# Summing stage and the tail of the expert stage: the margins are zeroed first, gathers and row statistics stand earlier in the queues, and ScalarE's order in a chunk is changed

## What is computed

```python
x = x + _layernorm(_L0_ffn_ref(_layernorm(x), ...))     # experts
x = x + _layernorm(_L1_attn_ref(_layernorm(x), ...))    # state space

# end of the experts: a token's four expert outputs, weighted, and the shared part
routed = einsum('ne,nef,efd->nd', comb, g * u, wd)
return routed + shared

# start of the state-space layer
proj = x @ W_in.T
val, gate, Bp, Cp, dt = split(proj, ...)
vc = conv_general_dilated(val, conv_w, padding=[(3, 0)])   # 4 taps, causal
val = silu(vc + conv_b)
```

## Time and profile before

| | |
|---|---|
| median of 3 runs | 1275.85 us (1274.46 to 1279.34) |
| profiled execution | 1269.8 us, of which the span is 1268.0 us |
| PE, PEld busy | 88%, 72% of the span |
| DVE, ACT, POOL busy | 69%, 50%, 30% of the span |
| expert stage | ends at 504.57 us |
| summing stage | 504.8 to 631.0 us |
| busy in the summing stage, by engine | PE 58 to 80%, DVE 39 to 87% of its parts |
| TensorE clock granted | 0.93 over the span, 0.72 to 0.84 in the summing stage |

### The profile page before, as it was taken

The page is one execution under the profiler, slowest core; times in us unless marked ns, Lnnn a source line. Parts: engine busy times, 40 slices in busy tenths (PEclk is TensorE's granted clock), DMA queues, the critical chain, the costliest instruction groups (busy, mean ns, idle before and its releaser), DMA issues. The chain is left out here.

```text
span 1268.0 us, 31644 instructions
## 1 busy us (share of the span) xinstructions
PE 1115.9 (88%) x12161; PEld 915.7 (72%) x12161; DVE 871.2 (69%) x2188; ACT 630.3 (50%) x1433; POOL 386.6 (30%) x561
## 2 busy tenths in 40 slices
PE   6569998689989993676799999999999999999987
PEld 5446776577778993455557888888888888888776
DVE  6467896877846776685476677667766776664574
ACT  4434456232333663476644554555455555553654
POOL 3331222176700265672055016202620261000120
PEclk9869999777999996777899999999999999999998
DMA  6748884222289885463243234223342332232001
GB/s 175 187 118 223 214 232 176 104 82 89 84 325 419 300 301 169 124 184 119 100 102 102 85 111 125 85 85 114 122 151 89 116 116 87 91 102 80 1 18 50
DMA packets 77986, 176.17 MB, mean 139 GB/s; under 512 B 12614, under 2 KB 26182, under 8 KB 75270
## 3 DMA queue, kind: packets, MB, share of 16 engines
q1 hardware_dynamic: 71564, 157.09, 38.6%
q0 software_dynamic: 6272, 17.05, 4.4%
HBM read 112.82 MB, written 61.08 MB: 137 GB/s over the span
## 5 line engine op out<-in xcount | busy, mean ns | idle before, releaser
L2378 ACT ACTIVATE decay<-masked,negcum 128x128 f32<-128x128 f32 x512 | 163.0, 391 | 101.8 <-DVE mixT L2442 101.8
L2286 PE MATMUL joint<-xh,w_high 128*128 128x512 f32 x512 | 209.3, 409 | 2.0 <-POOL wl L2222 2.0
L2286 PE MATMUL joint<-xl,w_high 128*128 128x512 f32 x512 | 200.2, 391 | 0.0
L2286 PE MATMUL joint<-xh,wl 128*128 128x512 f32 x512 | 199.9, 390 | 0.0
L2490 DVE COPY cT<-joint 128x512 f32<-128x512 f32 x128 | 88.3, 690 | 85.9 <-PE joint L2286 85.6
L2396 ACT ACTIVATE bT<-joint 128x512 f32<-128x512 f32 x128 | 76.7, 599 | 131.1 <-PE joint L2286 131.1
L2442 DVE TENSOR_TENSOR mixT<-pcb,decay 128x512 f32<-128x512 f32 x128 | 82.5, 685 | 55.7 <-PE pcb L2302 55.6
L2219 POOL TENSOR_TENSOR w_high<-w_in,none 128x512 fp32r<-128x512 f32 x32 | 36.1, 1127 | 260.7 <-DMA w_in<-in_w_bc 251.3
L2286 PEld LDWEIGHTS joint<-xh,w_high 128*128 128x128 f32 x512 | 96.2, 188 | 23.7 <-POOL wl L2222 2.4
L2286 PEld LDWEIGHTS joint<-xh,wl 128*128 128x128 f32 x512 | 96.1, 188 | 20.8
L2286 PEld LDWEIGHTS joint<-xl,w_high 128*128 128x128 f32 x512 | 96.3, 188 | 17.0
(11 more groups left out here) (367 smaller groups left out, 2717.3 us busy)
## 6 DMA issues: line engine op xcount, KB each, us to landing
cumrow<-ssm_cum SPq DMA_DIRECT2D x128, 256.0 KB, 3.2
slots_in<-blank SPq DMA_DIRECT2D x16, 1024.0 KB, 5.3
rows<-slots_in SPq DMA_DIRECT2D x32, 512.0 KB, 5.4
slots_out<-spare SPq DMA_DIRECT2D x32, 512.0 KB, 4.2
weights<-in_expert_quads SPq DMA_DIRECT2D x16, 768.0 KB, 8.8
w_in<-in_w_bc SPq DMA_DIRECT2D x32, 256.0 KB, 3.8
qk_parts<-parts SPq DMA_DIRECT2D x32, 192.0 KB, 2.3
stack<-qk_parts SPq DMA_DIRECT2D x32, 192.0 KB, 5.2
```

What stands on the lines that cost most here:

```text
L2286: last = nc.tensor.matmul(bank[:], w[:, j, col:col + P], a[:, k, c * CHUNK:(c + 1) * CHUNK], start=(m == 0), stop=(m == len(parts) - 1))
L2378: last = nc.scalar.activation(decay[:, n % 2, o], masked[:, n % 2, o], ACT.Exp, bias=negcum[:, c * TPC + i, head:head + 1])
```

## The change

It moves instructions and adds or removes no computation.

```diff
-EARLY_FROM, EARLY_EACH = 24, 2
+EARLY_FROM, EARLY_EACH = 23, 2
-COMBINE_AT = [26, 28, 30, 32]
+COMBINE_AT = [25, 27, 29, 31]
@@ stage_slots, GpSimd
                         for n in range((g - EARLY_FROM) * EARLY_EACH, (g - EARLY_FROM + 1) * EARLY_EACH):
+                            if n == TPC * TOPK:
+                                stored(1)
                             fetch(n)
-                stored(1)
-                late = list(range(TPC * TOPK, EARLY_TILES * TOPK))
-                for n in late[:4]:
+                for n in range((NQ - EARLY_FROM) * EARLY_EACH, EARLY_TILES * TOPK - 2):
                     fetch(n)
                 deviations(OF_Y)
-                for n in late[4:6]:
+                for n in range(EARLY_TILES * TOPK - 2, EARLY_TILES * TOPK):
                     fetch(n)
                 deviations(OF_X)
-                for n in late[6:]:
-                    fetch(n)
@@ stage_slots, VectorE, in the loop over the quads
+                    if g == NQ - 1:
+                        for part in w_copied:
+                            dve.wait_ge(part, OVER // 2)
+                        dve.wait_ge(added, TPC * TOPK)
+                        statistics(y, OF_Y)
@@ stage_mid, GpSimd
+                nc.gpsimd.memset(pad[:, :, :, 0:TAPS - 1], 0.0).then_inc(padded, 1)
                 for i in range(EARLY_TILES, 9):
                     fetch(i)
                 link(nc.gpsimd.memset(power[:], -0.5))
-                nc.gpsimd.memset(pad[:, :, :, 0:TAPS - 1], 0.0).then_inc(padded, 1)
                 deviations(OF_Y, 1)
                 fetch(9)
                 deviations(OF_X, 1)
-                for i in range(10, 13):
+                for i in range(10, 15):
                     fetch(i)
                 deviations(OF_Y, 2)
-                fetch(13)
+                fetch(15)
                 deviations(OF_X, 2)
-                for i in range(14, NT):
-                    fetch(i)
@@ stage_mid, ScalarE
                 for c in range(LAST):
-                    take(c, range(CB_IN))
+                    take(c, range(CB_IN - 2))
                     for v in range(2):
                         silu(c, v)
+                    take(c, range(CB_IN - 2, CB_IN))
+                    normal_rows(c + 1)
                     for v in range(2):
                         values(c, v)
-                    normal_rows(c + 1)
                     high_part(c + 1)
```

More of the change, by code:

```diff
@@ L1430, in _ @@
                         for n in range((g - EARLY_FROM) * EARLY_EACH, (g - EARLY_FROM + 1) * EARLY_EACH):
+                            if n == TPC * TOPK:
+                                stored(1)
                             fetch(n)
-                for n in range((NQ - EARLY_FROM) * EARLY_EACH, TPC * TOPK):
-                    fetch(n)
                 pool.wait_ge(w_copied[1], OVER // 2)
                 link(nc.gpsimd.memset(norms["power"], -0.5))
-                stored(1)
-                late = list(range(TPC * TOPK, EARLY_TILES * TOPK))
-                for n in late[:4]:
+                for n in range((NQ - EARLY_FROM) * EARLY_EACH, EARLY_TILES * TOPK - 2):
                     fetch(n)
                 deviations(OF_Y)
-                for n in late[4:6]:
+                for n in range(EARLY_TILES * TOPK - 2, EARLY_TILES * TOPK):
                     fetch(n)
                 deviations(OF_X)
-                for n in late[6:]:
-                    fetch(n)
             @block.sync
```

## The result

The changed kernel takes 1267.04 us in the median of six runs (1262.39 to 1269.18). The kernel before, run on the same chip, took 1274.03 (1269.75 to 1279.34). The ratio is 0.9945, with a 95% interval of 0.9919 to 0.9970: faster by 0.55%. Forecast were 1269.7 us and a gain of 6.2. Measured against the runs beside it, the gain is 7.0; the kernel before had a median of 1275.85 in the three runs that the forecast started from and 1274.03 in six, which is 1.8 of the 2.7 us between forecast and result.

What follows compares the result with a forecast made beforehand. GpSimd's drain was taken to end the expert stage, a GpSimd-VectorE loop to pace the summing stage. Expert -6.2 and summing +0.1 + 0.3 - 0.4 = 0 took 1275.85 to 1269.7 us; range 1264.2 to 1275.6.

Steps and rivals of the forecast that it cites:

- VectorE: Expert stage: with the third combine no longer ahead of the last product, VectorE's statistics start 2.8 us earlier (1.8 to 3.3).
- The drain: End of the expert stage: with no gather behind the second power, GpSimd's drain ends 6.2 us earlier (4.2 to 8.3).
- rival A: Expert stage: drain length kept from the last instruction, dearer combines, plus cold clock in chunk 2: -3.5 us, 1272.4; chance 0.13.
- my three readings: Expert stage: GpSimd's drain end counted from the last issue (gain 7.8 or 5.3 us) or the last instruction (5.2).
- SyncE: Expert stage: SyncE's store is issued about 2 us later, harmless as its drain began some 10 us before the barrier's end.
- VectorE's 1.62 us: Summing stage, chunk 0 to 1: VectorE's wait for ScalarE goes, so chunk 1's power of `x` is done 1.4 us earlier.
- the wait of 5.70 us for tile 15: Summing stage, chunk 3: VectorE's wait vanishes and cancels chunk 2's delay of 5.8 us, leaving chunk 3's rows 0.1 later.
- ScalarE's order: Summing stage: two evictions follow the normalisation instead of filling its wait for GpSimd, costing 0.3 us.
- The clock: Summing stage: TensorE's granted clock in chunk 3's projection gains 0.4 us, bounds 1.9 gained to 1.9 lost.
- B: Summing stage: chunk 2's delay of 5.5 us isn't paid back, as TensorE and ScalarE set chunk 3: -0.7, 1275.2; chance 0.08.
- C: All bounds fall well: drain gain 7.8 and 1.7 us from TensorE's clock, -9.5, 1266.4; chance 0.08.
- D: Summing stage: VectorE stretches the 24 gathers ahead of chunk 2's powers; at 0.69 us each +10.3, 1286; chance 0.05.

Runs made afterwards that it cites:

- The two halves: Against the changed kernel, one half of the change set back as before: expert stage's change alone, ratio 0.9948; summing stage's change alone, ratio 0.9997.
- split gathers: Changed kernel with GpSimd's summing-stage gathers as 14 ahead of chunk 2's first power, 4 between, 6 behind: 1263.0 us, ratio 0.9928; with ScalarE's old order too, 1261.45, 0.9903.
- the one with 12, 4 and 8: Changed kernel with the gathers around chunk 2's powers as before: 12 ahead, 4 between, 8 behind; 1265.27 us, ratio 0.9929.
- the expert part alone: Changed kernel with the summing stage set back as before, only the expert stage's change kept: 1268.57 us, ratio 0.9948.

## Why the prediction was right

**The place of the gain: right.** It said -6.2 in the expert stage and 0 in the summing stage; the profiles have -5.8 and -0.3. The two halves run apart say the same (0.9948 and 0.9997). Counted from the opening of the stage at 355.19 in the profile of before, the barrier opens at 355.19 + 143.68 = 498.9; 498 to 499 was forecast.

**VectorE: right.** The statistics came 2.6 us earlier instead of 2.8. The last product starts 0.6 earlier (128.66 instead of 129.22 us into the stage; 0.7 forecast), directly behind the product and eviction of the quad before, and the last eviction with its wait, 2.1 us, is out of the way.

**The drain: mis-sized.** I took a gain of 6.2 for the second power's 2.8, the two gathers behind it and the drain's end, because part of a drain might be counted from the last gather. It isn't: with the last gather further ahead it stays 2280 ns. The reading that I gave rival A, a fixed tail behind the last instruction, was right. Only the tail is 2.0 us behind a small operation instead of the 2.8 behind a gather. None of my three readings had that; the 6.2 was a value between them, so that it comes this near is in part luck. The sum was 2.65 (the second power starts at 140.16 instead of 142.81 us into the stage) + 3.2 (from it to the barrier 502.54 - 499.02 = 3.5 us instead of 504.71 - 498.00 = 6.7) = 5.8. The run with the gathers put back bears out the 3.2. The run with the statistics put back lost 3.8 and not 2.65, but its statistics were 3.8 later: it bears out that they count one for one.

**SyncE: right.** Before, it had 10.6 us to spare ("some 10"). GpSimd's end came 5.8 earlier, and SyncE reached its drain 1.4 later (140.13 instead of 138.75 us into the stage; its store was put about 2 later), so 3.4 are left. In the run with the memset back they were 1.5. With that much more taken out of the end of GpSimd's queue, SyncE would be next.

**The summing stage: right, and by the steps named.** VectorE's 1.62 us went. Of the 20 gathers forecast 25.5 us (534.5 to 560.0), they took 558.75 - 532.67 = 26.1. The new wait is 5.02 us (about 5 forecast), the rows of chunk 2 come 5.9 later (5.5), and the wait of 5.70 us for tile 15 vanished. ScalarE's order was put at +0.3; with split gathers it measures nothing, and in the changed kernel one run isn't enough to say. The clock was put at 0.4 gained: over the same seven us of the stage it went from 0.62 to 0.66, 0.04 x 2 x 7 = 0.6 us less at the lower level and so 0.3 us of time. Over the 13.9 us of the earlier trace rows, counted from the stage's start, it went from 0.86 to 0.88.

**The rivals.** A (the tail counted from the last instruction) was right about the drain and wrong about the dearer combines; its -3.5 was too small. B (the 5.5 us of chunk 2 aren't paid back) falls: with the power early again, chunk 3's rows come 1.1 earlier and the stage is shorter by only 0.2. C asked for 1.7 us from the clock and 7.8 from the drain; neither came. D (gathers stretched by VectorE) falls: 26.1 / 20 = 1.30 us each against 1.27. Only the stage's first gather was long:

```profile
502.68 2.56 DVE L2001 TENSOR_TENSOR win_low<-win_raw,win_high 128x2304 fp32r<-128x2304 f32 x1 [3.75 <-PEq L1389]
```

```profile
503.57 2.55 POOL L1739 DMA_INDIRECT back<-slots_out,slots  x1 [0.56 <-issue]
```

It ends at 506.12, 0.88 us behind the VectorE instruction (505.24): the remainder of one instruction and about a gather's own 0.95. The Trainium skill (SBUF — State Buffer, "Who interferes with whom") says that a VectorE instruction with two SBUF inputs contends with a GpSimd instruction that reads SBUF, and, for VectorE's two-port modes, that whoever issues first holds the shared pair for the whole instruction. If that holds here, the loss is at most one instruction's rest for a gather, and both traces agree. It isn't shown: in all 14 profiles the stage's first gather starts 0.84 to 0.89 us into this instruction and lasts 2.50 to 2.58, so they can't tell a wait for VectorE from a first gather behind a barrier that is long for another reason.

The low end of my range, 1264.2, was not worked out: C's 1266.4 less the 1.4 between median and lowest run is 1265.0. Nothing rests on it.

**What stays open.** Whether the order of the gathers alone makes the changed kernel differ from the one with 12, 4 and 8: 1267.04 and 1265.27 have intervals that overlap. What sets the moment at which a gather of the summing stage lands, 2.7 to 5.0 us after the start of its issue. And what moves the start of the expert stage's statistics by up to 1.7 us under one code.

## What to carry to other kernels

A large wait is worth what waits behind it: 13.3 us of ScalarE's idle time (12.8 in the kernel before) were worth no more than 0.6 us of its stage, because the stage was paced by a loop of two other engines, while a pair of gathers that nobody needed in that stage, queued behind the last dependent step ahead of a barrier, were worth 3.2. On an engine that both issues transfers at a fixed price and takes part in a chain, count both due times: moving 8 gathers as a block ahead of a power only traded one wait for another of the same size, and splitting them around it made the stage 3.2 us shorter. Where a part of the program scatters by more than the effect sought (here the routing stage, by 5 us), compare stage by stage from barrier to barrier, and don't take the difference of two spans for the effect. Then look for the event that the stage's end follows at a fixed distance (here the statistics, 10.7 or 13.8 us ahead): it separates what the change did from what scattered.

## What the runs showed of the hardware that was not expected

- In the expert stage, which has gathers, GpSimd's drain ends a fixed time behind its last instruction. In ten kernels whose last instruction was the small operation it was 2278 to 2280 ns, 2.0 us behind that instruction's end, with the last gather 2.3 or 6.6 us ahead of the drain. In the four that ended on gathers it was 5437 to 5518 and ended 2.8 us behind the last issue, 1.03 behind the last landing. At the end of the summing stage, behind a DMA of GpSimd's queue from `z`, it was 4161 or 4162 each time.
- The routing stage with its scatters took 124.3 to 129.4 us with the same code and data.
- With the same code of the summing stage (the kernel before, its repeat, the expert part alone), VectorE's three waits for gathers were 6.5 to 6.6, 1.8 to 4.2 and 5.7 to 6.9 us. Over all profiles a gather of this stage landed 2.7 to 5.0 us after the start of its issue, which isn't a constant to plan with.
